# Adding the attention shift one batch ahead on GpSimd, behind VectorE's expert rows, in a transformer block with experts

## The chip, the cores and the metric

One NeuronCore of a Trainium2 chip. Its engines run their own instruction queues and meet through semaphores: TensorE (PE in the profile, weight loads PEld), VectorE (DVE), ScalarE (ACT), GpSimd (POOL), and SyncE (SP), which here only issues DMAs. The metric is the device time of one launch in microseconds.

## The reference

```python
mod = (silu(c) @ wmod)                      # per batch: sa, ca, ga, sb, cb, gb, 128 each
h = layernorm(x) * (1 + ca) + sa            # x: 8 batches x 1024 tokens x 128
x = x + ga * attention(h)                   # exp(tanh((hW+b) h^T * 1/|i-j|)), no diagonal, row-normalised, times h
h = layernorm(x) * (1 + cb) + sb
x = x + gb * ffn(h)                         # 8 experts, top 2 of 8, hidden 512, and one shared expert
```

Attention is applied to the normalised rows, and because the row weights sum to one the shift sa can be added afterwards: the kernel keeps x in SBUF (`res`), adds `ga*sa` to it (the shift), and later adds the scaled attention sum.

## The kernel before

**Tiling.** A batch is 128 partitions x 8 groups of 128 features (G = 8), so an elementwise instruction over a batch is 128x1024 f32. `res` holds all eight batches in SBUF. The attention part is a loop over batches b = 0 to 7, written out by hand for each engine; the expert part comes after it and runs over 47 tiles of sorted rows.

**One batch of attention.** Eight score tiles t, each 128 keys x 1024 queries. TensorE makes the scores, VectorE weighs them by distance (`weigh(b, t)`, L1238, one input in PSUM and one in SBUF, signals `score_used`), ScalarE takes tanh (L873) and exp (L875, `exp_done`), TensorE multiplies with the values (L1868, `value_step`). Between these, in a fixed order on each queue, lies the work of neighbouring batches:

- VectorE in batch b: `weigh` 0 and 1, `attend(b-1)` (L1247, takes the sums from PSUM), `take_ranks(b-2)` (L1308 and L1309; the latter adds two SBUF tensors of eight elements a partition), `scale_attended(b-1)` (L1256, L1257, L1260), `split_h` (L1188), `weigh` 2, `add_attended(b-1)` (L1269, which waits for `shift_added`), `moments_2(b-1)` (L1121, L1125), `split_h`, `weigh` 3, `split_q`, `normalise_2(b-1)` (L1225, waits for the second rstd), `weigh` 4, `assign(b-2)` (up to L1333, which signals `slots_ready`), `weigh` 5, `rows_for_experts(b-1)` (L1355 and L1359, the latter signals `ln2_h`; from b = 3 on), `weigh` 6 and 7, `shift_1(b+3)` (L1135, b = 3 and 4), `moments_1(b+4)` (b = 2 and 3), `choose(b-1)` (L1275, L1278, the searches L1282, and L1284) and `count_chosen` (L1290 to L1298).
- TensorE in batch b: scores 0 and 1, the last two value products of batch b-1, `ranks(b-2)` (L1889, L1890: once a batch), scores 2 and so on.
- GpSimd in batch b: `rstd_1(b+3)` in batches 3 and 4 (L528, and the pow L530; `ALU.pow` with -0.5), `add_shift(b)` (L596), then sixteen row scatters, each an indirect DMA issued by GpSimd (L622, "sends"), paced by `score_used` and `exp_done`. After the fifth comes `rstd_2(b-1)` (L600, and the pow L602), which VectorE's `normalise_2` waits for. Sends 0 to 7 carry rows of batch b-3, sends 8 to 15 rows of batch b-2; send 8 waits for `slots_ready`. In batch 2 GpSimd also makes the expert rows of batch 1 (L610, L617); from batch 3 on VectorE does.

`add_shift(b)` waits for `ln1_xhat` of batch b (ScalarE has read `res` for the normalised rows), which is over one batch earlier, and releases `shift_added`, which `add_attended(b)` needs in batch b+1. In the kernel before, `add_shift(b)` stands at the head of batch b for b = 2 to 6, and `add_shift(7)` in batch 6 between sends 11 and 12.

Of the kernel before, what the change touches and what calls it, by code (L numbers as in the profile page):

```python
# [35 lines left out]
B, S, D = 8, 1024, 128  # L36
G = S // P
# [80 lines left out]
def adaln_moe(nc, x, c_t, wmod, w_att, b_att, wg, packs, out):  # L118
    with ExitStack() as ctx:
# [6 lines left out]
        def sem(name):  # L126
            return ctx.enter_context(nc.semaphore(name))
# [185 lines left out]
        score_used = sem("score_used")  # L313
# [12 lines left out]
        ln2_h = sem("ln2_h")  # L326
# [196 lines left out]
        def _(pool):  # L523
            def rstd_1(b0, b1):

                pool.wait_ge(ln1_moments, b1)
                rs = rstd[:, b0 * G:b1 * G]
                nc.gpsimd.tensor_scalar(rs, moments[:, b0 * G:b1 * G, 1], EPS_LN, None, ALU.add).then_inc(ln1_pool_step, b1 - b0)  # L528
                pool.wait_ge(ln1_pool_step, b1)
                nc.gpsimd.tensor_tensor(rs, rs, minus_half[:, 0:(b1 - b0) * G], ALU.pow).then_inc(ln1_rstd, b1 - b0)  # L530
# [58 lines left out]
            def add_shift(b):  # L589

                pool.wait_ge(ln1_xhat, b + 1)
                if b == 0:
                    pool.wait_ge(ln1_half, 1)
                    pool.wait_ge(mod_loaded, 16)
                r = res[:, b * G:b * G + G, :]
                nc.gpsimd.tensor_tensor(r, r, mod[:, b:b + 1, 0, :].to_broadcast([P, G, D]), ALU.add).then_inc(shift_added, 1)  # L596

            def rstd_2(b):
                pool.wait_ge(ln2_moments, b + 1)
                nc.gpsimd.tensor_scalar(rstd2[:, :], moments2[:, :, 1], EPS_LN, None, ALU.add).then_inc(ln2_pool_step, 1)  # L600
                pool.wait_ge(ln2_pool_step, b + 1)
                nc.gpsimd.tensor_tensor(rstd2[:, :], rstd2[:, :], minus_half[:, 0:G], ALU.pow).then_inc(ln2_rstd, 1)  # L602

            def scale_rows(b):

                pool.wait_ge(ln2_xhat, b + 1)
                wait(pool, scattered[b % 2], 16 * 2 * G * (b // 2))
                wait(pool, second_rows, b - 1)
                scale = mod[:, b:b + 1, 3, :].to_broadcast([P, G, D])
                nc.gpsimd.tensor_tensor(rows_1[b % 2][:, :, 0:D], xhat2[:, :, :], scale, ALU.mult).then_inc(ln2_mod_step, 1)  # L610

            def shift_rows(b):

                pool.wait_ge(ln2_mod_step, b + 1)
                shift_ = mod[:, b:b + 1, 2, :].to_broadcast([P, G, D])
                to = rows_1[b % 2][:, :, 0:D]
                nc.gpsimd.tensor_tensor(to, to, shift_, ALU.add).then_inc(ln2_h, 1)  # L617
# [25 lines left out]
            def send_step(b, t, i):  # L643

                groups = sends(b, t)
                if i < len(groups):
                    send_one(*groups[i])
# [46 lines left out]
            def second_batch(b):  # L694
                rstd_2(b - 1)
                scale_rows(b - 1)
                shift_rows(b - 1)
                rstd_1(4, AHEAD)

            def batch(b, par):  # L700
                if b == 0:
                    rstd_1(2, 3)
                    add_shift(0)
                    rstd_1(3, 4)
                    add_shift(1)
                    return
                if b == 1:
                    return second_batch(b)
                if b == B - 1:
                    return last_batch(b)  # L710
                if AHEAD <= b + 3 < B:
                    rstd_1(b + 3, b + 4)
                pool.wait_ge(score_used, G * b + 1)
                add_shift(b)
                send_step(b, 0, 0)
                pool.wait_ge(exp_done, G * b + 1)
                send_step(b, 0, 1)
                pool.wait_ge(score_used, G * b + 2)
                send_step(b, 1, 0)
                pool.wait_ge(exp_done, G * b + 2)  # L720
                send_step(b, 1, 1)
                pool.wait_ge(score_used, G * b + 3)
                send_step(b, 2, 0)
                rstd_2(b - 1)
                if b < 3:
                    scale_rows(b - 1)
                pool.wait_ge(exp_done, G * b + 3)
                send_step(b, 2, 1)
                pool.wait_ge(score_used, G * b + 4)
                send_step(b, 3, 0)  # L730
                pool.wait_ge(exp_done, G * b + 4)
                send_step(b, 3, 1)
                pool.wait_ge(score_used, G * b + 5)
                send_step(b, 4, 0)
                pool.wait_ge(exp_done, G * b + 5)
                send_step(b, 4, 1)
                pool.wait_ge(score_used, G * b + 6)
                send_step(b, 5, 0)
                pool.wait_ge(exp_done, G * b + 6)
                send_step(b, 5, 1)  # L740
                if b < 3:
                    shift_rows(b - 1)
                pool.wait_ge(score_used, G * b + 7)
                if b == B - 2:
                    add_shift(b + 1)
                send_step(b, 6, 0)
                pool.wait_ge(exp_done, G * b + 7)
                send_step(b, 6, 1)
                pool.wait_ge(score_used, G * b + 8)
                send_step(b, 7, 0)  # L750
                pool.wait_ge(exp_done, G * b + 8)
                send_step(b, 7, 1)
# [9 lines left out]
            modulation()  # L762
            rstd_1(1, 2)
            batches(pool, batch)
            order = iter([(B - 3, m) for m in range(3 * (G - FIRST), 2 * G)] + [(b, m) for b in (B - 2, B - 1) for m in range(2 * G)])

# [1453 lines left out]
```

## Time and profile before

| | us |
|---|---|
| three runs, median (lowest to highest) | 642.19 (642.18 to 644.39) |
| the profiled execution, its own time | 641.25 |
| span of its profile | 639.5 |
| busy in the span: PE, DVE, ACT, POOL | 613.3, 459.0, 406.3, 350.3 |
| granted TensorE clock, mean | 0.992 |
| attention part, batches 0 to 7 | about 17 to 275 |
| shift addition L596, eight times | 2.36 to 2.40 each |

A row of the timeline has: start in us from the span's start, duration in us, engine, line, operation, output<-inputs by the program's names, shapes, and in brackets the idle time before it with what ended it. On VectorE the recorded start of an instruction lies some 0.08 us before the recorded end of the one ahead of it when they follow without a gap. A row of the chain of waits has start, duration and what the end of the program depended on in that stretch.

### The profile page before, as it was taken

Reading aid. Unit: us, or ns where it says so; the run is one execution under the profiler, and the core shown is the slowest. Engines: PE = TensorE matmul, PEld = TensorE weight load, DVE = VectorE, ACT = ScalarE, POOL = GpSimd, SP = SyncE. Lnnn points to the kernel's source line nnn. Section 1 sums busy time; section 2 is a strip of 40 time slices with the busy share of each in tenths; the row PEclk is TensorE's granted clock in tenths of the full one; section 3 lists DMA queues with packets and bytes.
Section 4 is the critical chain, followed back from the end, with each engine's and each line's share of the span. In section 5 each row is a group of like instructions: output and inputs, shape, how many; then the busy total and the mean of one; then the engine's idle time right before and its main releaser. Section 6 shows DMA issues by size and latency. Waiting matters only on the chain.

```text
span 639.5 us, 13351 instructions
## 1 busy us (share of the span) xinstructions
PE 613.3 (96%) x4339; PEld 557.5 (87%) x4339; DVE 459.0 (72%) x1425; ACT 406.3 (64%) x647; POOL 350.3 (55%) x347
## 2 busy tenths in 40 slices
PE   7899999999999998969999999999999999999997
PEld 5788898788888887858999999999999999998897
DVE  7869798999989896966842676665556544452598
ACT  3698778778787876725565656665555656463551
POOL 5450526867666666665763565566656556466100
PEclk8999999999999999988999999999999999999999
DMA  7500000110111111110752555567666566521793
GB/s 295 196 14 1 2 2 18 34 35 30 34 34 35 34 35 38 39 46 25 243 168 83 180 180 182 184 187 213 182 205 192 183 189 191 177 68 31 268 403 128
DMA packets 30031, 76.46 MB, mean 120 GB/s; under 512 B 7142, under 2 KB 11646, under 8 KB 29856
## 3 DMA queue, kind: packets, MB, share of 16 engines
q1 hardware_dynamic: 20624, 58.49, 28.1%
q0 software_dynamic: 8640, 16.93, 7.9%
q8 instruction: 23, 0.38, 0.3%
q10 hardware_dynamic: 720, 0.47, 0.2%
q14 instruction: 24, 0.20, 0.1%
HBM read 53.53 MB, written 23.24 MB: 120 GB/s over the span
## 4 chain that ended last, share of the span: by engine, by line
PE 60%; DVE 22%; ACT 5%; issue 5%; POOL 3%; another core or an unknown queue 3%; DMA 1%; POOLq 0%; SPq 0%; DVEq 0%; ACTq 0%
PE value L2060 24%; PE score L1840 8%; PE score L1842 8%; PE score L1841 8%; PE value L1868 6%; DVE work L1238 4%; DVE rows_all L1225 2%; DVE stats L1121 2%; PE value L2108 2%; PE misc L1882 2%; ACT work L873 2%; DVE rows_all L1260 2%; ACT work L875 2%; POOL rstd L602 1%
## 5 line engine op out<-in xcount | busy, mean ns | idle before, releaser
L817 POOL DMA_INDIRECT rows_z<-tile_y,tags x138 | 142.4, 1032 | 101.1 <-issue 43.7
L1840 PE MATMUL score<-h_hi,h_lo 128*128 128x512 f32 (+1 forms) x252 | 94.4, 374 | 0.3 <-ACT work L904 0.2
L1868 PE MATMUL value<-w_ring,work 128*128 128x129 f32 x768 | 93.2, 277 | 0.8 <-ACT work L875 0.3
L1868 PEld LDWEIGHTS value<-w_ring,work 128*128 128x128 f32 x768 | 89.8, 192 | 4.7 <-ACT work L875 2.0
L873 ACT ACTIVATE work<-work 128x1024 f32<-128x1024 f32 x64 | 67.3, 1052 | 38.3 <-DVE work L1238 36.2
L1842 PE MATMUL score<-h_hi,h_lo 128*128 128x512 f32 (+1 forms) x252 | 89.4, 355 | 0.0
L904 ACT ACTIVATE work<-score,w_ring 128x512 f32<-128x512 f32 (+1 forms) x96 | 53.2, 617 | 55.7 <-PE score L1842 41.8
L622 POOL DMA_INDIRECT rows_x<-work,slot x64 | 65.7, 1027 | 35.0 <-issue 16.9
L1238 DVE TENSOR_TENSOR work<-score,lw 128x1024 f32<-128x1024 f32 x64 | 76.6, 1215 | 5.0 <-remote 2.3
L1841 PE MATMUL score<-h_hi,h_lo 128*128 128x512 f32 (+1 forms) x220 | 76.4, 347 | 0.0
L2060 PE MATMUL value<-w_ring,work 128*128 128x128 f32 x640 | 75.4, 275 | 0.0
L2060 PEld LDWEIGHTS value<-w_ring,work 128*128 128x128 f32 x640 | 73.3, 192 | 0.0
L875 ACT ACTIVATE work<-work 128x1024 f32<-128x1024 f32 x64 | 67.8, 1060 | 2.0
L904 ACT ACTIVATE work<-score,rows_all 128x256 f32<-128x256 f32 (+1 forms) x92 | 44.4, 550 | 36.3 <-PE score L1842 33.4
L904 ACT ACTIVATE work<-score,w_shared 128x512 f32<-128x512 f32 x64 | 40.2, 686 | 42.7 <-PE score L1842 23.0
L1840 PE MATMUL score<-q_hi,h_lo 128*128 128x512 f32 x128 | 55.3, 432 | 5.5 <-DVE work L1238 4.5
L2060 PE MATMUL value<-rows_all,work 128*128 128x128 f32 x464 | 55.4, 275 | 0.0
L2060 PEld LDWEIGHTS value<-rows_all,work 128*128 128x128 f32 x464 | 53.6, 192 | 0.1
L1842 PEld LDWEIGHTS score<-h_hi,h_lo 128*128 128x128 f32 x252 | 47.7, 189 | 6.7
L1840 PEld LDWEIGHTS score<-h_hi,h_lo 128*128 128x128 f32 x252 | 47.9, 190 | 6.0 <-issue 0.8
L2060 PEld LDWEIGHTS value<-w_shared,work 128*128 128x128 f32 x384 | 46.1, 197 | 5.1 <-issue 4.4
L1842 PE MATMUL score<-q_hi,h_hi 128*128 128x512 f32 x128 | 50.4, 394 | 0.0
(282 smaller groups left out, 1208.4 us busy)
## 6 DMA issues: line engine op xcount, KB each, us to landing
w_ring<-packs SPq DMA_DIRECT2D x24, 578.0 KB
rows_all<-packs SPq DMA_DIRECT2D x23, 578.0 KB
lw<-rows_x SPq DMA_DIRECT2D x24, 260.0 KB
res<-x SPq DMA_DIRECT2D x8, 512.0 KB, 6.5
h_t<-rows_z SPq DMA_DIRECT2D x3, 1024.0 KB, 11.7
mod<-mod_rows SPq DMA_DIRECT2D x1, 2560.0 KB, 8.8
rows_z<-tile_y,tags POOLq DMA_INDIRECT x142
rows_all<-rows_z SPq DMA_DIRECT2D x2, 1024.0 KB, 13.2
```

The costliest lines, as they stand in the source:

```text
L622: nc.gpsimd.indirect_dma_start(rows_x[:, :], bass.IndirectOffsetOnAxis(ap=slot[b % 2][:, k, g:g + 1], axis=0), (rows_1, rows_2)[k][b % 2][ ...
L817: nc.gpsimd.indirect_dma_start(rows_z[:, :], bass.IndirectOffsetOnAxis(ap=tags[pos][:, k, 0:1].bitcast(I32), axis=0), tile_y[par][:, k, :] ...
L873: nc.scalar.activation(prob[:, t % 4, :], prob[:, t % 4, :], ACT.Tanh).then_inc(tanh_done, 1)
L875: nc.scalar.activation(prob[:, t % 4, :], prob[:, t % 4, :], ACT.Exp).then_inc(exp_done, 1)
L904: ins = nc.scalar.activation(hidden[par][:, c, 0:rows], score[:, c, 0:rows], ACT.Relu, bias=w[:, B1_AT + c:B1_AT + c + 1])
L1121: ins = nc.vector.bn_stats(st[:, g, :], res[:, bass.ds(b * G + g, 1), :].rearrange("p o d -> p (o d)"))
L1238: nc.vector.tensor_tensor(prob[:, t % 4, :].rearrange("p (h n) -> p h n", h=2), score[:, 2 * (t % 2):2 * (t % 2) + 2, :], lw[:, at:at + S] ...
L1840: nc.tensor.matmul(out, a_lo, b_hi, start=True, stop=False)
L1841: nc.tensor.matmul(out, a_hi, b_lo, start=False, stop=False)
L1842: return nc.tensor.matmul(out, a_hi, b_hi, start=False, stop=True)
L1868: ins = nc.tensor.matmul(value[:, s // 3, c0:c0 + D + 1], prob[:, t % 4, s * P:(s + 1) * P], normal[b % 3][:, t, :], start=(t == 0 and s % ...
L2060: ins = nc.tensor.matmul(bank[:, k * D:(k + 1) * D], hidden[part][:, c, k * P:(k + 1) * P], w[:, W2_AT + c * D:W2_AT + (c + 1) * D], start ...
```

## The change

GpSimd's queue only. The shifts of batches 0, 1 and 2 stay. The shift of batch 3 is added in batch 2 between sends 11 and 12, behind the shift of the expert rows (L617) and the wait for the seventh score. The shifts of batches 4 to 7 are added in batches 3 to 6, at the same place between sends 11 and 12, behind a wait for `ln2_h` of count b (VectorE has made the expert rows of batch b-1), and ahead of the wait for the seventh score.

```diff
                 pool.wait_ge(score_used, G * b + 1)
-                add_shift(b)
+                if b == 2:
+                    add_shift(b)
                 send_step(b, 0, 0)
...
                 send_step(b, 5, 1)
                 if b < 3:
                     shift_rows(b - 1)
+                    pool.wait_ge(score_used, G * b + 7)
+                else:
+                    pool.wait_ge(ln2_h, b)
+                if b < B - 1:
+                    add_shift(b + 1)
                 pool.wait_ge(score_used, G * b + 7)
-                if b == B - 2:
-                    add_shift(b + 1)
                 send_step(b, 6, 0)
```

## Rows read from the trace of the kernel before

**Rows 1.** Timeline of PE: the ranks matmul, once in batches 3 to 6.
```profile
117.17 0.29 PE L1889 MATMUL misc<-prefix,before 128*128 128x8 f32 x2
...
151.22 0.29 PE L1889 MATMUL misc<-prefix,before 128*128 128x8 f32 x2
...
184.20 0.29 PE L1889 MATMUL misc<-prefix,before 128*128 128x8 f32 x2
...
216.15 0.29 PE L1889 MATMUL misc<-prefix,before 128*128 128x8 f32 x2
```

**Rows 2.** Chain that ended last, in order of time, batches 3 and 4.
```profile
121.54 1.92 DVE rows_all L1260 x7
...
152.91 1.12 DVE carry L1309
...
169.84 2.05 PE value L1868 x16
```

**Rows 3.** All of line L1309: duration ns min/median/max, first and last start.
```profile
L1309 DVE TENSOR_TENSOR carry<-carry,prefix x8: 159/174/2062, 86.2 to 313.2; 128x8 f32<-128x8 f32 x8
```

**Rows 4.** Timeline of POOL, end of batch 2 and batch 3.
```profile
109.30 2.20 POOL L617 TENSOR_TENSOR work<-work,mod 128x1024 f32<-128x1024 f32 x1
...
118.53 2.36 POOL L596 TENSOR_TENSOR res<-res,mod 128x1024 f32<-128x1024 f32 x1
121.06 1.10 POOL L622 DMA_INDIRECT rows_x<-rows_all,slot  x1 [0.18 <-issue]
...
125.20 1.96 POOL L622 DMA_INDIRECT rows_x<-rows_all,slot  x1 [0.30 <-issue]
127.47 0.96 POOL L622 DMA_INDIRECT rows_x<-rows_all,slot  x1 [0.30 <-issue]
128.78 0.58 POOL L600 TENSOR_SCALAR rstd<-moments 128x8 f32<-128x8 f32 x1 [0.35 <-DVE moments L1125]
...
142.05 0.96 POOL L622 DMA_INDIRECT rows_x<-work,slot  x1 [0.30 <-issue]
```

**Rows 5.** Timeline of POOL, batches 0, 1, 4 and 6.
```profile
37.15 1.67 POOL L530 TENSOR_TENSOR rstd<-rstd,minus_half 128x8 f32<-128x8 f32 x1
...
62.71 0.24 POOL L600 TENSOR_SCALAR rstd<-moments 128x8 f32<-128x8 f32 x1 [21.53 <-DVE moments L1125]
...
151.62 2.38 POOL L596 TENSOR_TENSOR res<-res,mod 128x1024 f32<-128x1024 f32 x1
...
238.96 0.96 POOL L622 DMA_INDIRECT rows_x<-row,slot  x1 [0.30 <-issue]
239.94 2.38 POOL L596 TENSOR_TENSOR res<-res,mod 128x1024 f32<-128x1024 f32 x1
```

**Rows 6.** Timeline of DVE, batch 0 and batches 2 to 4.
```profile
37.91 0.68 DVE L1188 TENSOR_TENSOR h_lo<-tile_y,h_hi 128x512 fp32r<-128x512 f32 x1
...
112.57 0.15 DVE L1284 TENSOR_TENSOR gap<-top_v 128x8 f32<-128x8 f32 x1
...
117.44 1.36 DVE L1247 TENSOR_TENSOR rows_all<-value,rows_all 128x387 f32<-128x387 f32 x3 [0.79 <-PE value L1868]
...
118.85 2.06 DVE L1309 TENSOR_TENSOR carry<-carry,prefix 128x8 f32<-128x8 f32 x1
...
125.11 1.22 DVE L1269 TENSOR_TENSOR res<-res,rows_all 128x1024 f32<-128x1024 f32 x1
...
128.60 0.66 DVE L1188 TENSOR_TENSOR h_lo<-tile_y,h_hi 128x512 fp32r<-128x512 f32 x1
...
137.09 0.17 DVE L1333 TENSOR_SCALAR token_no<-token_no 128x8 f32<-128x8 f32 x1
...
143.10 0.16 DVE L1135 SCALAR_TENSOR_TENSOR shift<-moments,rstd 128x8 f32<-128x8 f32 x1
...
152.83 1.20 DVE L1309 TENSOR_TENSOR carry<-carry,prefix 128x8 f32<-128x8 f32 x1
...
178.25 0.23 DVE L1275 COPY logits<-misc 128x64 f32<-128x64 f32 x1 [1.99 <-PE misc L1882]
```

## Prediction

> **What bounds the kernel now.** I read the page first: the busy shares name TensorE, but those are means over an attention part and an expert part, and the change touches only the attention part of batches 2 to 6. So the next view is the timeline of TensorE, taken at one matmul that occurs once a batch (the ranks, L1889). The reader is to see its spacing [rows 1]: 34.05 us from batch 3 to 4, 32.98 from 4 to 5, 31.95 from 5 to 6. If 31.95 is the pace that the rest of the work allows, the two earlier batches lose 2.10 and 1.03 us, 3.13 together. That is the cap of what removing anything in them can bring.
>
> Who loses them is in the chain of waits [rows 2]: from 121.54 it runs over VectorE, with one odd piece, 1.12 us for the carry addition L1309, and comes back to TensorE's values at 169.84. The VectorE timeline then shows L1309, eight elements a partition, taking 2.06 us in batch 3 and 1.20 in batch 4 [rows 6], against 0.17 in the median of its eight runs [rows 3]. What ran beside it is in the GpSimd timeline: the shift addition L596 from 118.53 to 120.89 [rows 4] and from 151.62 to 154.00 [rows 5]. L1309 ends at 120.91 and 154.03, within 0.03 us of L596's end both times. So a VectorE instruction with both inputs in SBUF stands still until GpSimd's long addition is over. Cost: 2.06 - 0.16 = 1.90 us and 1.20 - 0.16 = 1.04 us, close to the losses of 2.10 and 1.03. In the later batches GpSimd has no rstd of a later batch ahead of L596, which then comes and goes before L1309.
>
> **The change, part by part.** The eight additions stay; none is added. Moved are shifts 3, 4, 5, 6 and 7.
>
> *Shift 7.* It stood behind the wait for the seventh score already, and GpSimd arrives there late: its last send ends at 239.92 and L596 starts at 239.94 [rows 5]. The new wait (VectorE's expert rows) is over before. Nothing changes: 0.
>
> *Shifts 5 and 6* leave the head of batches 5 and 6 and go behind the sixth pair of sends in batches 4 and 5. No L1309 is blocked there now; the sends get 2.4 us later at the tail and 2.4 earlier at the head. The tail has room: the sends of one batch are read by TensorE only much later. 0.
>
> *Shift 3* leaves 118.53 and goes behind L617, which ends at 111.50 [rows 4]; it then runs to 113.9. GpSimd is busy without a gap from there to 121.06, so this only permutes its queue: four sends to 118.9, the rstd of batch 6 to 120.9, first send of batch 3 at 121.06 as before. Removed: L1309's 1.90 us. Added: VectorE's L1284 at 112.57 [rows 6] has both inputs in SBUF and now waits until 113.9, 1.3 us. Of that 0.79 is covered by VectorE's idle wait for TensorE ahead of L1247 at 117.44 [rows 6]; 0.5 stays. VectorE's scaling L1260 is thus 1.9 - 0.5 = 1.4 us earlier. But what is late next is GpSimd. VectorE's normalise_2 (L1225) needs the second rstd, and this stands behind five sends. Now VectorE's moments arrive at 128.7, and the last of the five sends ends at 128.43 [rows 4]: a margin of 0.3. With moments at 127.3, GpSimd is the later one. Its five sends at a pitch of 0.96 + 0.30 from 121.06 would end at 127.1. Yet a send beside the VectorE addition L1269 (125.11 to 126.33) took 1.96 instead of 0.96 [rows 4, 6], so 1.0 is added, and smaller brushes of 0.1 to 0.4 by the other two-input instructions. I lay the five beside VectorE's new times: 0.1 + 0.1 + 1.04 + 0 + 0.4, end 128.75. The rstd then runs free of L1188, which in the run before stretched L600 to 0.58 (128.78, beside L1188 from 128.60; free 0.24) [rows 4 to 6]. L600 to 129.0 and the pow of 1.67 behind it [rows 5] to 130.8, against 129.36 and 131.1 before. Gain of batch 3: 0.35 us, between 0 (the sends brush more) and 0.75 (the last one doesn't).
>
> *Shift 4* leaves 151.62 and goes behind the sixth pair of batch 3, whose last send ends at 143.01 [rows 4]. Removed: 1.04 us at L1309 of batch 4. The same test of GpSimd: L596 from 143.03 to 145.4, four sends to 150.4, the rstd of batch 7 to 152.4, all 0.35 earlier, instead of the 154.00 at which L596 ended; five sends at the pitch of 1.26 and a brush or wait of 1.5 to 2 then end at 159.9 to 160.3. The moments came 7.8 us behind the end of L1309 in batch 3 (120.91 to 128.7); in batch 4 it now ends at 154.03 - 1.04 - 0.35 = 152.6, so they come at 160.4. So here VectorE leads, barely, and the 1.04 is kept. L1309 itself is clear of GpSimd: the rstd of batch 7 is over at 152.0 and L1309 comes at 152.83 - 0.35 = 152.5.
>
> *The new neighbour.* Behind that last send (143.01) the addition starts after 0.02 us, at 143.03. VectorE's shift_1 (L1135), both inputs in SBUF, starts at 143.10 [rows 6], and both hang on the same release, the slots of L1333 at 137.09, so their distance stays 0.07 us whatever moved earlier. Who takes the port first? L600 started at 128.78, was let go when L1188 ended at 129.26, and ended at 129.36; with 0.24 for a free one it asked for the port about 0.14 us after its start. So L596 would ask near 143.17, and L1135 in 143.10 to 143.26. This can't be decided from the trace. If VectorE is first, GpSimd waits 0.1 us: nothing. If GpSimd is first, L1135 waits to 145.4, costs 2.17 us, and behind it on VectorE are the moments of batch 7, the choice, and the scores of batch 4. The same pair meets in batch 4 (shift 5), but there VectorE then waits 1.99 us for TensorE anyway, until 178.25 [rows 6], and the addition is over at 178.4: 0 to 0.2, in slack.
>
> **Sum.** Likeliest: 0.35 + 1.04 = 1.4 us less. The profiled execution took 641.25 (span 639.5), so it would take 639.9. The median of the runs is 642.19, 0.94 above it: 640.8.
>
> **Rule and row.** Rows: GpSimd's pow L530 ran from 37.15 to 38.82, and VectorE's L1188 at 37.91, both inputs in SBUF, took its usual 0.68 [rows 5, 6]; so GpSimd's eight-element pow doesn't hold VectorE to its end. The Trainium skill (SBUF — State Buffer, Who interferes with whom) says that the one to issue first holds the shared port pair for the whole instruction. L1309 agrees; the pow doesn't. By that rule L1260 would stand behind the pow in batch 3 (rival 3).
>
> **Rivals.**
> 1. *L1135 loses the race (slower than before).* Place: batch 3, behind the last of the twelfth send. +2.17 at L1135, -1.04 at L1309 of batch 4, -0.35 of batch 3: +0.8 us, 643.0; without the 0.35, 643.3. It decides once GpSimd asks for the port before VectorE does, a matter of 0.05 us. For it: L596's earlier recorded start. Against: L1135 touches only eight elements.
> 2. *The sends don't slow GpSimd.* Then VectorE's whole 1.4 of batch 3 arrives: -(1.4 + 1.04) = -2.5, 639.7. Against: the send of 1.96 us. The same page infers that a two-input VectorE addition leaves descriptor generation alone; by it this would be the result, and the 1.96 beside L1269 speaks against it.
> 3. *The pow takes the place of the addition.* The rstd of batch 6 now lies at 119.2 to 120.9, where L596 lay. If it holds L1260 until then, batch 3 gains 0 and batch 4 its 1.04: 641.2. Against: 37.91 above.
> 4. *Nothing moves:* the pace of batches 3 and 4 has another cause, and L1309's wait lies in slack: 642.2. Against: L1309 is on the chain.
>
> **Chances and range.** Forecast 0.45, rival 1 0.34, rival 2 0.06, rival 3 0.07, rival 4 or a mixture 0.08. Range 639.5 to 643.6: from rival 2 to rival 1 without its 0.35, with 0.2 to 0.3 for the scatter of a median; about 0.8 is in it. The range of the forecast itself: 640.4 (0.75 in batch 3) to 641.2 (0). A measurement of this kernel tells from no change about 0.5%, 3.2 us; that is more than the cap of 3.13, and slower by as much would take rival 1 with its 2.17 unpaid and more. Faster by over 0.5% 0.05, within 0.88, slower by over 0.5% 0.07.
>
> **What would show it.** L1309 at 0.16 to 0.25 in batches 3 and 4. L1284 in batch 2 at 1.4 us. The spacings of L1889: 33.7 from batch 3 to 4, 31.95 from 4 to 5, with the forecast; 33.7 and 34.1 with rival 1. L1135 of batch 3: 0.16, or 2.3. The send beside L1269 in batch 3 again near 2 us, and L602 there no more than 0.4 us earlier against L1889. The prediction fails if another two-input instruction of VectorE meets the addition (the searches L1282 just ahead of L1284, which no row shows beside one), or if TensorE's clock dips elsewhere.

## The result, and the profile after

| | before, beside it | after | ratio, 95% interval |
|---|---|---|---|
| median (lowest to highest), us | 643.29 (642.18 to 644.64) | 652.13 (650.73 to 652.85) | 1.0134 [1.0102, 1.0166] |

The change makes the kernel slower by 1.3%, some 9 us. The forecast was 1.4 us less, with 643.6 as the upper end. The profiled execution took 652.85 us (span 651.1, mean granted clock 0.980) against 641.25 (639.5, 0.992). Medians here and below hold all executions of a kernel, while the ratios leave out the disturbed ones. In the kernel after every line number behind the diff is 4 higher: L1893 is the ranks matmul that was L1889, L1313 the carry addition L1309, L1139 the shift computation L1135, L1251 the line that takes the attention sums (L1247).

First the timeline of PE after, at the ranks matmul, batches 3 to 7, against [rows 1]:

```profile
118.29 0.29 PE L1893 MATMUL misc<-prefix,before 128*128 128x8 f32 x2
...
152.68 0.36 PE L1893 MATMUL misc<-prefix,before 128*128 128x8 f32 x2 [0.20 <-DVE prefix L1302]
186.45 0.29 PE L1893 MATMUL misc<-prefix,before 128*128 128x8 f32 x2
...
221.69 0.29 PE L1893 MATMUL misc<-prefix,before 128*128 128x8 f32 x2
...
258.73 0.28 PE L1893 MATMUL misc<-prefix,before 128*128 128x8 f32 x2
```

| from rank to rank, us | 3 to 4 | 4 to 5 | 5 to 6 | 6 to 7 |
|---|---|---|---|---|
| before | 34.05 | 32.98 | 31.95 | 31.56 |
| after | 34.39 | 33.77 | 35.24 | 37.04 |
| more | 0.34 | 0.79 | 3.29 | 5.48 |

The 1.12 us by which batch 3 already starts later (118.29 against 117.17) lie ahead of the change's reach: the ranks of batch 2 are already 1.11 us later (85.72 against 84.61). The batches that the prediction argued over cost 1.1 us. The loss is in batches 5 and 6, 8.8 us, which it priced at nothing.

The timeline of DVE after shows the part that was foreseen, and the loss, against [rows 6]:

```profile
113.65 1.30 DVE L1288 TENSOR_TENSOR gap<-top_v 128x8 f32<-128x8 f32 x1
...
120.08 0.16 DVE L1313 TENSOR_TENSOR carry<-carry,prefix 128x8 f32<-128x8 f32 x1
...
131.49 2.17 DVE L1229 TENSOR_SCALAR rows_all<-res,moments,rstd 128x128 f32<-128x128 f32 x8 [1.11 <-POOL rstd L602]
...
143.44 2.35 DVE L1139 SCALAR_TENSOR_TENSOR shift<-moments,rstd 128x8 f32<-128x8 f32 x1
...
156.11 0.21 DVE L1313 TENSOR_TENSOR carry<-carry,prefix 128x8 f32<-128x8 f32 x1
...
189.48 1.36 DVE L1251 TENSOR_TENSOR rows_all<-value,w_ring 128x387 f32<-128x387 f32 x3 [2.70 <-remote]
...
226.10 1.36 DVE L1251 TENSOR_TENSOR rows_all<-value,rows_all 128x387 f32<-128x387 f32 x3 [4.95 <-remote]
```

L1313 is free now, 0.16 instead of 2.06 us in batch 3 and 0.21 instead of 1.20 in batch 4; L1288 pays 1.30. L1139 takes 2.35 us instead of 0.16. And VectorE stands still for 2.70 and 4.95 us ahead of L1251, which waits for the last value product of the batch. "Remote" means that the profile finds no instruction that ended when the wait did. The timeline of PE says that the product was finished long before:

```profile
182.88 3.74 PE L1872 MATMUL value<-w_ring,work 128*128 128x129 f32 x32
...
188.06 0.39 PE L1846 MATMUL score<-q_hi,h_hi 128*128 128x512 f32 x1
191.11 0.63 PE L1827 MATMUL misc<-ident,w_ring 128*128 128x128 f32 x4 [2.67 <-DVE place L1312]
```

The value products end at 186.62 by the records, but the signal of the last one arrives at 189.45, and VectorE goes on at 189.48. In the semaphore events of the trace, which carry the time at which each signal arrives, the rank signal of batch 5 comes 3.21 us behind the recorded end of its matmul and that of batch 6 3.94 us; before, both were 0.01 us behind. The score signal that follows the rank signal comes 0.74 us after it in batch 5, and 0.08 us after it in batch 6 (226.22 against 226.14), while the matmuls between the two take 1.49 us by their records both times. So it looks as if TensorE worked on time and its signals came late. The ends of matmuls are modelled in this trace, so a real standstill inside TensorE for a part of the time isn't excluded. Signals of VectorE and ScalarE aren't late at these places.

What GpSimd does there is in the timeline of POOL after, batches 4 and 5, and 5 and 6, against the pattern of [rows 4]:

```profile
178.29 2.38 POOL L596 TENSOR_TENSOR res<-res,mod 128x1024 f32<-128x1024 f32 x1
180.84 0.98 POOL L622 DMA_INDIRECT rows_x<-row,slot  x1 [0.17 <-issue]
182.13 0.96 POOL L622 DMA_INDIRECT rows_x<-row,slot  x1 [0.30 <-issue]
183.39 0.96 POOL L622 DMA_INDIRECT rows_x<-row,slot  x1 [0.30 <-issue]
184.66 0.96 POOL L622 DMA_INDIRECT rows_x<-row,slot  x1 [0.31 <-issue]
185.92 0.96 POOL L622 DMA_INDIRECT rows_x<-rows_all,slot  x1 [0.31 <-issue]
188.10 0.96 POOL L622 DMA_INDIRECT rows_x<-rows_all,slot  x1 [1.22 <-ACT work L879]
...
213.53 2.39 POOL L596 TENSOR_TENSOR res<-res,mod 128x1024 f32<-128x1024 f32 x1
216.08 0.98 POOL L622 DMA_INDIRECT rows_x<-work,slot  x1 [0.17 <-issue]
...
223.74 0.96 POOL L622 DMA_INDIRECT rows_x<-work,slot  x1 [0.30 <-issue]
```

The addition in the tail makes GpSimd 2.4 us late, so the four sends of the tail wait for nothing any more. At the head of the next batch, where the addition used to stand between tail and head, the sends go straight on. Five follow each other without a pause at 180.84 to 186.88, and seven at 216.08 to 224.70. In batch 5 the signal of the last but one value product, due at 184.83, arrives at 187.94, 1.06 us after the run; those behind it, the last value product's at 189.45 among them, come while two more sends go (188.10 to 190.33). In batch 6, where none follow, the last value, rank and score signals arrive together at 226.08 to 226.22, 1.4 to 1.5 us after the run.

The view by windows of 2 us shows what comes behind it. Its columns are the window and its length, the busy time of PE, PEld, DVE, ACT and POOL (with the number of instructions), the granted clock of TensorE as a share of full speed, the DMA share and GB/s:

```profile
188.00:190.00 2.00, 0.45 (x2) 0.02 (x1) 0.52 (x2) 0.00 (x0) 1.59 (x2) 1.00 0.10 33
190.00:192.00 2.00, 0.89 (x8) 0.92 (x9) 1.93 (x10) 0.22 (x1) 0.33 (x1) 0.96 0.10 33
192.00:194.00 2.00, 2.00 (x11) 2.00 (x11) 2.00 (x8) 1.97 (x3) 0.00 (x0) 0.50 0.00 0
194.00:196.00 2.00, 2.00 (x10) 1.78 (x10) 2.00 (x3) 1.97 (x3) 0.00 (x0) 0.69 0.00 0
196.00:198.00 2.00, 2.00 (x11) 1.65 (x10) 1.97 (x9) 1.97 (x3) 1.22 (x2) 1.00 0.00 0
```

TensorE is idle for 2.67 us, and from 191.8 to 195.3 the clock is 1.2 instead of 2.4 GHz; in batch 6 TensorE is idle for 4.04 us, and the clock is at the lower level for 6.8 us. The value products that start at 191.58 take 3.40 us where the same sixteen took 1.95 in the kernel before, 1.45 us more. So each wait is paid a second time behind it. Slack takes up a part: VectorE's waits of 2.70 and 4.95 us come with distances that are 3.29 and 5.48 us longer. The Trainium skill (TensorE: Matmul & The Clock Gate, HAM oscillation — how this bites in real kernels) says that idle gaps of TensorE bring the lower clock and that it is paid behind each gap; the rows agree.

### The profile page after: what moved, and what is told of

It reads as the page before. It is cut to its first block, busy times and chain, and to the rows that moved or that the text cites. A ratio compares the mean times of both kernels' runs of the same rounds, so it can differ in the third digit from the quotient of the medians.

```text
span 651.1 us, 13355 instructions
## 1 busy us (share of the span) xinstructions
PE 618.0 (95%) x4339; PEld 562.3 (86%) x4339; DVE 461.6 (71%) x1425; ACT 406.3 (62%) x647; POOL 347.9 (53%) x347
## 4 chain that ended last, share of the span: by engine, by line
PE 59%; DVE 24%; issue 5%; POOL 5%; ACT 3%; another core or an unknown queue 2%; DMA 1%; DVEq 0%; POOLq 0%; SPq 0%
PE value L2064 23%; PE score L1844 8%; PE score L1846 8%; PE score L1845 8%; PE value L1872 6%; DVE work L1242 4%; POOL rows_x L622 2%; PE value L2112 2%; DVE rows_all L1229 2%; DVE stats L1125 1%; DVE top_i L1286 1%; PE misc L1827 1%; PE misc L1886 1%; DVE rows_all L1251 1%
## 5 line engine op out<-in xcount | busy, mean ns | idle before, releaser
L1872 PE MATMUL value<-w_ring,work 128*128 128x129 f32 x768 | 94.6, 279 | 0.6 <-ACT work L879 0.3
L1872 PEld LDWEIGHTS value<-w_ring,work 128*128 128x128 f32 x768 | 91.6, 195 | 3.9 <-ACT work L879 1.7
L622 POOL DMA_INDIRECT rows_x<-work,slot x64 | 63.9, 999 | 44.6 <-issue 16.6
L2064 PEld LDWEIGHTS value<-w_ring,work 128*128 128x128 f32 x640 | 73.3, 192 | 0.0
L1845 PE MATMUL score<-q_lo,h_hi 128*128 128x512 f32 x128 | 50.3, 393 | 0.0
```

The lines of the kernel that those rows point to most:

```text
L622: nc.gpsimd.indirect_dma_start(rows_x[:, :], bass.IndirectOffsetOnAxis(ap=slot[b % 2][:, k, g:g + 1], axis=0), (rows_1, rows_2)[k][b % 2][ ...
L1845: nc.tensor.matmul(out, a_hi, b_lo, start=False, stop=False)
L1872: ins = nc.tensor.matmul(value[:, s // 3, c0:c0 + D + 1], prob[:, t % 4, s * P:(s + 1) * P], normal[b % 3][:, t, :], start=(t == 0 and s % ...
L2064: ins = nc.tensor.matmul(bank[:, k * D:(k + 1) * D], hidden[part][:, c, k * P:(k + 1) * P], w[:, W2_AT + c * D:W2_AT + (c + 1) * D], start ...
```

## The experiments

The kernels ran on four chips in turn, called A to D here; which of them, if any, the result above is from isn't known. Each was compared with the kernel before on its own chip, and only so are the times to be read:

| runs | chip | before there, us | kernel, us | ratio, 95% interval |
|---|---|---|---|---|
| 1 only shift 3 ahead | A | 641.63 | 641.60 | 1.0007 [0.9989, 1.0024] |
| 2 only shift 4 ahead | A | 641.63 | 644.14 | 1.0039 [1.0014, 1.0065] |
| 3 only shifts 5 and 6 ahead | A | 641.63 | 648.75 | 1.0125 [1.0101, 1.0150] |
| 4 all ahead, one send later | A | 641.63 | 644.12 | 1.0060 [1.0038, 1.0081] |
| 5 shifts 5 and 6 in halves | B | 641.95 | 642.62 | 1.0019 [0.9996, 1.0042] |
| 6 run 3 with a held send | B | 641.95 | 644.02 | 1.0026 [1.0005, 1.0046] |
| 7 shifts 5 and 6 tiny | B | 641.95 | 642.19 | 1.0006 [0.9982, 1.0031] |
| 8 a run of six sends, nothing moved | B | 641.95 | 644.93 | 1.0041 [1.0020, 1.0061] |
| 9 shift 7 at its head | C | 631.88 | 635.37 | 1.0054 [1.0034, 1.0075] |
| 10 run 9, shifts 3 and 4 ahead and later | C | 631.88 | 633.10 | 1.0016 [1.0003, 1.0029] |
| 11 the changed kernel again | C | 632.65 | 632.37 | 1.0012 [0.9994, 1.0030] |
| 12 the kernel before again | C | 632.65 | 632.44 | 0.9999 [0.9978, 1.0019] |
| 13 run 9 again | C | 632.65 | 635.30 | 1.0048 [1.0031, 1.0064] |
| 14 run 10 again | C | 632.65 | 633.25 | 1.0015 [1.0003, 1.0027] |
| 15 the changed kernel, third time | D | 647.00 | 663.10 | 1.0236 [1.0187, 1.0286] |
| 16 shifts 3 and 4 ahead, one send later | D | 647.00 | 646.92 | 0.9995 [0.9974, 1.0016] |
| 17 run 16, shift 7 in halves | D | 647.00 | 643.66 | 0.9960 [0.9937, 0.9984] |

**Which part costs (runs 1 to 4).** Theory A: the sends close up into a run, and that makes TensorE's signals late. Theory B: the wait of L1139 sets the later batches back. In runs 1 to 3 only some shifts are moved, with the change's place and waits:

```diff
                 pool.wait_ge(score_used, G * b + 1)
-                add_shift(b)
+                if b not in (5, 6):
+                    add_shift(b)
...
+                if b + 1 in (5, 6):
+                    if b < 3:
+                        pool.wait_ge(score_used, G * b + 7)
+                    else:
+                        pool.wait_ge(ln2_h, b)
+                    add_shift(b + 1)
                 pool.wait_ge(score_used, G * b + 7)
```

(3 or 4 in place of 5, 6 in the other two.) In run 4 all additions of the change stand behind send 12 instead of send 11. What was expected:

> Only the shift of batch 3 goes ahead (into batch 2). The result of the whole change is 8.8 us slower than before, and its trace shows three things: L1135 (L1139 after) of batch 3 stands 2.35 us beside the moved addition; TensorE's value_step and rank signals of batches 5 and 6 come some 3 and 4 us behind the recorded matmuls while GpSimd issues five to seven row sends in a row; and then the granted clock falls to one half. Theory A (runs of sends): what costs is that the addition no longer stands between the sends of one batch's end and the next one's head; this one here isn't such a place, since the rstd of batch 6 still stands there, so 0 to 0.5 us less than before. Theory B (VectorE's block): what costs begins with L1135 beside the addition in batch 3; shift 3 doesn't touch it, so the same 0 to 0.5 us less. L1309 of batch 3 falls from 2.06 to 0.2 us, L1284 of batch 2 rises from 0.15 to 1.3.

> Only the shift of batch 4 goes ahead (into batch 3). Theory A: plus 2.2 us at L1135, minus 1.04 at L1309 of batch 4, so about 1.1 us slower than before and no more; the clock doesn't fall in batches 5 and 6. Theory B: VectorE's block alone starts the later losses, so most of the 8.8 us.

> Only the shifts of batches 5 and 6 go ahead. Theory A: nearly the whole loss, 7 to 9 us slower than before, with TensorE's signals late at the start of batches 5 and 6 and the clock at one half behind it. Theory B: L1135 of batch 4 is blocked, in slack; 0 to 0.5 us, no fall of the clock.

> The whole change, but each addition one send later (behind the seventh pair's first send), so that L1135 is over before it starts. Theory A: the sends behind it are still followed by the next batch's without a break, so still 6 to 8 us slower than before. Theory B: L1135 is free, so 1 to 2 us faster than before.

Shift 3 alone changes nothing that can be measured in the time. Shift 4 alone costs 2.5 us, where 1.1 was expected (the interval, 0.9 to 4.2 us, holds both). Its L1142 (L1135 in the kernel before) takes 2.35 us at 143.84, the later batches keep their distances of 31.91 and 31.57 us, and no rank signal of batches 5 and 6 is late: the wait of that line alone doesn't start the loss, and theory B falls. Shifts 5 and 6 alone cost 7 us, most of the 8.8. Timeline of DVE in run 3:

```profile
187.23 1.36 DVE L1254 TENSOR_TENSOR rows_all<-value,w_ring 128x387 f32<-128x387 f32 x3 [2.68 <-remote]
...
223.33 1.36 DVE L1254 TENSOR_TENSOR rows_all<-value,rows_all 128x387 f32<-128x387 f32 x3 [4.95 <-remote]
```

The same two waits as in the changed kernel to 0.02 us, from rank signals 3.17 and 3.94 us late. Run 4 leaves one send fewer behind each addition, so that four sends go in a row in batch 5 and four in batch 6, and the same waits shrink to 1.07 and 2.08 us. Its time fits neither theory: A wanted 6 to 8 us more than before, B 1 to 2 less, and it is 2.5 more. Theory A was too high for a run that is only one or three sends shorter.

**The run of sends, or the missing addition (runs 5 to 8).** Theory C: it costs that the addition is gone from the head, whatever the sends do. Run 5 adds four groups ahead and four at the head. Run 6 is run 3 with one more wait. Run 7 leaves the additions at their heads but adds only eight elements a partition of shifts 5 and 6. Run 8 moves no addition and only holds sends back, so that they go in a row:

```diff
 run 6, at the head of batches 5 and 6
+                if b in (5, 6):
+                    pool.wait_ge(score_used, G * b + 2)
                 send_step(b, 0, 0)
 run 8, in the tail of batches 4 and 5
+                if b in (4, 5):
+                    pool.wait_ge(score_used, G * b + 8)
                 send_step(b, 5, 0)
```

> Shifts 5 and 6 cut into two halves of four groups each, one half ahead (between sends 11 and 12 of the batch before), the other at the head of its own batch. Theory A (five or more sends in a row, with no other work between them, make TensorE's signals late): the half at the head parts the sends of the tail, four in a row, from those of the head. No late rank signal (lag under 1 us, where the kernel with shifts 5 and 6 ahead had 3.17 and 3.94), no half clock in batches 5 and 6, time within 1 us of the kernel before, 641 to 643. Theory C (what costs is that the addition is gone from the head, whatever the sends do): half of it is gone, so about half of the 7 us that both cost, 645.

> Shifts 5 and 6 ahead as in the run that cost 7 us, and in batches 5 and 6 the first send of the batch is held until VectorE has weighed the second score tile, with nothing else put in its place. Theory A: the hold parts the run of sends, four in the tail and then a pause of some 2 us, so the rank signal is on time and the time is 641 to 644. If a pause is not enough and it takes other work of GpSimd, or if the missing addition itself costs (theory C): 648 to 649 and a lag of 3 to 4 us as before the hold.

> The shift additions of batches 5 and 6 stay at the head of their batch but add only eight elements a partition (the rest of these two shifts is left out). GpSimd has 2.2 us less work there and nothing more in the tail. Theory A: without the late addition in the tail the sends go at the pace of the scores, no run of five forms across the border, no late signal: 641 to 642. Theory C: the long addition is gone from the head as in the changed kernel, so the same loss: 648 to 649.

> All additions stay where the kernel before has them; in batches 4 and 5 sends 10 and 11 are held until VectorE has weighed the eighth score tile, so that the last six sends of the batch go in a row, up to the addition at the head of the next. Theory A: the run alone, with no addition moved, makes the rank signals of batches 5 and 6 late by 3 us or so; each costs about 3 us, and the clock may fall behind it: 646 to 649. Theory C: nothing was moved; only the carry addition is brushed for 0.4 us: 642 to 643.

Runs 5 and 7 are level with the kernel before, and no rank signal of batches 5 and 6 is late in run 5; for run 7 the trace shows it for batch 5 and the undisturbed distances (31.94 and 31.55 us) for both. In run 5 a piece of work of 1.28 us, with 1.55 us from the send ahead of it to the send behind it, is enough. Run 6 is a pause alone. Timeline of POOL in run 6, batches 5 and 6:

```profile
185.38 0.96 POOL L622 DMA_INDIRECT rows_x<-rows_all,slot  x1 [1.94 <-DVE work L1247]
...
216.62 0.96 POOL L622 DMA_INDIRECT rows_x<-work,slot  x1 [1.07 <-DVE work L1247]
```

The pause of 1.94 us mends batch 5 (rank signal 0.01 us late). That of 1.07 us in batch 6 doesn't: the rank signal is 2.52 us late and VectorE waits 2.87 us. So a pause can do what work does; whether 1.07 us of work would be enough wasn't tried. Theory A wanted run 8 at 646 to 649 and signals 3 us late; it got 644.93. Timelines of POOL and DVE in run 8:

```profile
177.25 0.96 POOL L622 DMA_INDIRECT rows_x<-row,slot  x1 [3.47 <-DVE work L1240]
...
183.56 0.96 POOL L622 DMA_INDIRECT rows_x<-row,slot  x1 [0.31 <-issue]
184.54 2.40 POOL L596 TENSOR_TENSOR res<-res,mod 128x1024 f32<-128x1024 f32 x1
```

```profile
186.01 1.36 DVE L1249 TENSOR_TENSOR rows_all<-value,w_ring 128x387 f32<-128x387 f32 x3 [2.12 <-PE value L1870]
```

The value signals arrive at 185.83 and 185.99, 1.3 and 1.5 us after the sixth send ended at 184.52, and VectorE stands still for 2.12 us in batch 5 and 2.15 in batch 6, with every addition at its head. The run alone does it; theory C (642 to 643 here, 648 to 649 for run 7) falls. By the records the signal that L1249 waits for is only 1.30 us late and the rank signal 1.0, since here the run ends before the matmuls do; the first of the two value signals, due at 182.91, is 2.92 us late. That suggests that the price goes by how far the run reaches past them. The kernel before bears it out: it has five sends in a row in the middle of its batches too (138.04 to 144.28, 171.04 to 177.28, 203.02 to 209.26). The signal of the logits matmul L1882 behind them comes at 145.28, 178.22 and 210.20, 0.94 to 1.00 us after the run, but the matmul itself ends only then, and the signal is 0.7 to 0.8 us late. The number of sends alone doesn't set the price.

**A better version, and a surprise (runs 9 to 14).** In the kernel before, shift 7 already stands in the tail. Its timelines of POOL and DVE, not shown so far:

```profile
239.94 2.38 POOL L596 TENSOR_TENSOR res<-res,mod 128x1024 f32<-128x1024 f32 x1
242.48 0.99 POOL L622 DMA_INDIRECT rows_x<-row,slot  x1 [0.17 <-issue]
...
248.86 0.96 POOL L622 DMA_INDIRECT rows_x<-rows_all,slot  x1 [0.30 <-issue]
```

```profile
249.63 1.23 DVE L1238 TENSOR_TENSOR work<-score,lw 128x1024 f32<-128x1024 f32 x1 [2.14 <-remote]
```

Six sends in a row and a wait of 2.14 us for a score signal, with the rank signal 2.81 us late: the kernel before has the same late signals in batch 7. Run 9 is to part that run of sends by putting shift 7 at the head of batch 7, and run 10 adds shifts 3 and 4 ahead, behind send 12.

> The kernel before with one move the other way: shift 7, which stood in batch 6 between sends 11 and 12, goes to the head of batch 7. Theory A: in the kernel before, this addition makes GpSimd late too, and the six sends behind it (242.48 to 249.82) run on into batch 7, where the rank signal lagged 2.81 us and VectorE stood still 1.10 and 2.14 us. With the addition between the tail's sends and the head's, the signals are on time and VectorE's two waits shrink: about 2 us less, 640 where the kernel before takes 642. If the long run of fourteen sends at the end of batch 7 then starts later and takes it back: no change.

> Shift 7 at the head of batch 7 as well, and of the change only shifts 3 and 4 ahead, each one send later than the change puts it (behind send 12), where the run with all additions one send later had no long wait of the shift computation in batch 3 and distances of 33.53 and 31.97 us between ranks against 34.05 and 32.98. Shifts 5 and 6 stay at their heads, so no run of sends forms. Expected: 0.5 and 1.0 us from batches 3 and 4 on top of what shift 7 at its head gives, 3 to 3.5 us together by theory A, 638.5; if the move of shift 7 gives nothing, 640.5.

Both missed: 3.5 and 1.2 us slower. But they ran on chip C, where the kernel before takes 631.9 us, and in neither trace is any TensorE signal more than 0.5 us late, not even behind fourteen sends. There is nothing to gain there, and the addition at the head of batch 7 holds a two-input instruction of VectorE for 2.42 us (L1290 at 247.59). So the changed kernel, the kernel before and both of these were run again:

> The changed kernel once more, unaltered, beside the kernel before. In the last call the kernel before took 631.9 us, 10 us less than on the two chips before it, and no TensorE signal in either kernel's trace came late, not even behind a run of fourteen sends. Theory A, as widened: whether signals come late behind a run of sends is a property of the chip. If this chip's kernel before takes about 642: lags of 3 to 4 us in batches 5 and 6 and 9 to 10 us more than before. If it takes about 632: no lag, and only the work of VectorE and GpSimd is left, with the shift computation of batch 3 held for 2.35 us: 0 to 2 us more than before. Theory D (the lags belong to the kernel and the last two runs only had a lucky order): lags here whatever the level of the kernel before.

> The kernel before itself, for a trace on this chip. If it takes about 642: the rank signal of batch 7 is 2.8 us late and that of the batch after 3.7 us. If it takes about 632: no signal late, spacings of the ranks in batches 6 and later near 31.5, 30.7 and 27, and all the 10 us lie behind 240 us. The ratio to itself shows what a comparison can tell: within 0.3% of one.

> Shift 7 at the head of batch 7 again. On a chip whose signals come late behind runs of sends, theory A gives 1 to 3 us less than the kernel before, since the run of six sends is parted; on one where they don't, 3 us more as in the last call, where the addition at the head held VectorE's two-input instruction for 2.42 us at 247.59.

> Shift 7 at the head, shifts 3 and 4 ahead behind send 12, again. With late signals: 2 to 4 us less than before; without: 0 to 1.5 us more, as in the last call.

It was chip C again, and on it the changed kernel is level with the kernel before, 1.0012 [0.9994, 1.0030]. Theory D (the late signals belong to the kernel) falls. Runs 13 and 14 repeat 9 and 10, as expected without late signals (2.7 and 0.6 us more than before). Timelines of POOL and DVE in run 11:

```profile
176.80 2.39 POOL L596 TENSOR_TENSOR res<-res,mod 128x1024 f32<-128x1024 f32 x1
179.36 0.98 POOL L622 DMA_INDIRECT rows_x<-row,slot  x1 [0.17 <-issue]
...
184.45 0.95 POOL L622 DMA_INDIRECT rows_x<-rows_all,slot  x1 [0.32 <-DVE work L1242]
```

```profile
142.66 2.36 DVE L1139 SCALAR_TENSOR_TENSOR shift<-moments,rstd 128x8 f32<-128x8 f32 x1
...
185.22 1.35 DVE L1251 TENSOR_TENSOR rows_all<-value,w_ring 128x387 f32<-128x387 f32 x3
```

The same run of five sends, the same hold of L1139, and L1251 starts without a wait. From rank 5 on the kernels keep the same pace: 32.01, 31.50 and 29.78 us in run 11, 32.12, 31.76 and 29.78 in run 12.

**A fourth chip (runs 15 to 17).** Run 16 is run 10 without the move of shift 7. Run 17 adds shift 7 in two halves, one at its old place and one at the head of batch 7:

```diff
                 if b == B - 2:
-                    add_shift(b + 1)
+                    add_half(b + 1, 0)
                 send_step(b, 6, 0)
+                if b + 1 in (3, 4):
+                    add_shift(b + 1)
...
             def last_batch(b):
                 pool.wait_ge(score_used, G * b + 1)
+                add_half(b, 4).then_inc(shift_added, 1)
                 send_step(b, 0, 0)
```

> The changed kernel a third time. Late signals come on some chips (kernel before near 642) and not on the last one (near 632). If the kernel before takes about 642 here: 9 us more than it, with rank signals 3 to 4 us late in batches 5 and 6. If about 632: within 0.3% of it and no late signal. A mix (before at 642 and the changed kernel without late signals, or the reverse) would speak against the chip as the cause.

> Of the change only shifts 3 and 4, each behind send 12 of the batch before instead of behind send 11; 5 to 7 as in the kernel before. On the last chip this with shift 7 at its head stood 2.0 us below shift 7 at its head alone (633.25 against 635.3), so without that head 2 us less than the kernel before: ratio 0.997. The same is expected where signals come late, since no run of sends is lengthened.

> As the run with shifts 3 and 4 behind send 12, and shift 7 in two halves of four groups, one where it stood (between sends 11 and 12 of batch 6), one at the head of batch 7. Where signals come late, the half at the head parts the run of six sends: 1 to 2 us less than without it. Where they don't: the half holds VectorE's two-input instruction by up to 1.2 us and nothing is gained, 0 to 1.5 us more than without it.

On chip D the kernel before takes 647.0 us and the changed kernel 663.1, 2.4% or 16 us more, where 9 was expected; its rank signals are 4.05 and 4.02 us late. Timeline of DVE in run 15:

```profile
191.91 1.36 DVE L1251 TENSOR_TENSOR rows_all<-value,w_ring 128x387 f32<-128x387 f32 x3 [4.21 <-remote]
...
229.57 1.36 DVE L1251 TENSOR_TENSOR rows_all<-value,rows_all 128x387 f32<-128x387 f32 x3 [5.04 <-remote]
```

Here even five sends cost 4.21 us, against 2.70. Run 16 gains nothing (0.9995); 0.997 had been expected. Behind the six sends of batch 7 its VectorE waits 3.63 us, as the kernel before presumably does on this chip (it has no trace from there). Run 17 parts those six. Timelines of DVE at that place, first run 16, then run 17:

```profile
249.89 1.22 DVE L1241 TENSOR_TENSOR work<-score,lw 128x1024 f32<-128x1024 f32 x1 [3.63 <-PE score L1845]
```

```profile
245.15 1.23 DVE L1248 TENSOR_TENSOR work<-score,lw 128x1024 f32<-128x1024 f32 x1 [2.06 <-PE score L1852]
246.51 1.31 DVE L1301 TENSOR_TENSOR hot<-expert_no,top_f 128x64 f32<-128x64 f32 x1
```

The rank signal, 2.94 us late in run 16, is on time (0.01), though VectorE's wait only falls to 2.06 us. The time falls from 646.92 to 643.66 us, more than the 1 to 2 us that were expected, and is below the kernel before at 0.9960 [0.9937, 0.9984]. It costs a hold of 1.31 us at L1301, so on a chip like C it should gain nothing; it wasn't run there.

## Why the prediction was wrong

**The step that failed** is the one on shifts 5 and 6: "the sends get 2.4 us later at the tail and 2.4 earlier at the head. The tail has room: the sends of one batch are read by TensorE only much later. 0." Who reads the sent rows doesn't matter. The two halves of the first sentence together close the gap between tail and head, and behind the run of five to seven sends TensorE's signals come 3 to 4 us late (run 3); where the run is parted they don't (run 5), and where it is made without moving an addition they do (run 8, up to 2.9 us). Measured: 3.3 and 5.5 us in the two batches, 7 us for both shifts alone on chip A, nothing that shows on chip C. The price went with the chip, which no reading of one trace could tell. That there was a price could be read: the "remote" wait of 2.14 us behind the six sends of batch 7 stood in the trace of the kernel before, behind the one addition that already stood where the change puts the others. The prediction looked at shift 7 only to say that it doesn't move; it was the sample of what the place costs.

**The race at L1135** went to rival 1. L596 starts at 143.37, L1139 0.07 us later at 143.44, and is held for 2.35 us (2.17 was the forecast's price, 2.19 measured over its 0.16). It is so in all three traces of the changed kernel, in batches 3 and 4, and in run 2. The step gave this 0.34 and should have given it more: the earlier recorded start decided, and the 0.14 us that L600 was thought to need before it asks for the port didn't save L1135. The Trainium skill (SBUF — State Buffer, Who interferes with whom) says that issue order decides who is held, and the traces agree here. The Trainium skill also has it there, of the SBUF ports, that TensorE never waits on anyone; the late signals of runs 3, 8 and 15 don't decide that, but they say that an engine waiting for TensorE can be held past the recorded end of its matmul.

**Rival 1's sum** was +0.8 us. In the kernel after, batches 3 and 4 cost 0.34 + 0.79 = 1.13 us. The hold in batch 4 is in slack, as the prediction said: in run 3 L1142 takes 2.34 us at 176.13, and the distance from rank 4 to 5 stays 32.97. The hold in batch 3 falls into both distances, so that rival 1's 33.7 and 34.1 came as 34.39 and 33.77. On chip C, where nothing else is in the way, the rank of batch 5 is 0.51 us later in run 11 than in run 12 (184.98 against 184.47), and the whole kernel 0.12% or 0.8 us slower (0.0012 × 632.65), with an interval from -0.4 to +1.9. The sum fits, but can't be told from zero, so that it fits to the tenth is luck.

**Batch 3's terms** came as worked out: L1309 free (0.16), L1284 held for 1.30, the send beside L1269 stretched (1.68 us at 124.80), and GpSimd the later one, since VectorE's L1229 now waits 1.11 us for the rstd [rows 4, 6]. The gain of 0.35 can't be read off by itself, because the hold of L1139 falls into the same distance: +0.34 in the changed kernel, +0.10 on chip C (34.06 against 33.96). With the hold taken out by placing the addition one send later, the distance is 33.53 in run 4 and 33.49 in run 16, 0.5 under the 34.05 of before. Run 1, which moves shift 3 alone to the place of the change, has 33.37, 0.68 less. So 0.35 was on the low side, within the 0 to 0.75 that was given.

**Batch 4's term**, 1.04 us, was right in kind. In run 4 the distance is 31.97 and in run 16 32.01, against 32.98. The 1.5 us of both don't show in the time of run 16, though (0.9995, at most 0.26% less). In the comparison of runs 13 and 14, which differ by these two moves alone, they do: 635.30 against 633.25. Where they go on chip D isn't settled, since the kernel before has no trace from that chip.

**Rivals 2, 3 and 4** aren't borne out: the sends did slow GpSimd down, the work did move, and the pow didn't hold VectorE (in batch 3 it runs from 120.25 to 121.92, and L1264 beside it, from 120.59 on, takes its usual 2.19 us). None of the rivals held the loss; rival 1 had the sign, but short by a factor of ten and more where signals come late.

**Open.** What makes TensorE's signals late isn't known. It needs indirect DMAs in a row, most of its late signals arrive 1 to 1.5 us after them, and it differs from chip to chip. A load of instructions doesn't explain it: in the changed kernel the trace has none between 179.02 and 202.51 us, and the signals of batch 5 are late from 184.83 to 190.91. Each chip was met on one or two occasions only, so that something else that differed between the occasions isn't excluded. Whether sends from another queue would do the same wasn't tried.

## What to carry to other kernels

When work is moved along a queue, look at both ends for what it stood between: here an addition parted two groups of DMA sends, and the closed-up run cost three times the two waits that were to be removed (8.8 us against 1.90 + 1.04), though on one chip of four nothing. If one member of a group already stands at the new place, read what happens around it before taking it for proof that the place is free; a wait whose releaser the profile can't name is a cost and belongs in the sum. Where a filler parts such a run, splitting it in halves can keep the run parted (runs 5 and 17). And compare on more than one chip before a gain or a loss of a per cent is called the kernel's.

## What the runs showed of the hardware

- Behind unbroken runs of GpSimd's indirect DMAs (0.96 us each, 1.26 us apart) TensorE's signals arrive late. Six in a row: 2.81 us late on the rank signal in the kernel before, seven: 3.94 in the changed kernel. Five: 3.21 there, 4.05 on chip D. The lateness isn't set by the number alone: behind five in the middle of a batch the signal of L1882 is only 0.7 to 0.8 us late, since its matmul ends after the run. Most of those that are held come in 1.0 to 1.5 us after the run ends. VectorE's and ScalarE's signals were on time. A break of 1.55 us with 1.28 us of other work, or a pause of 1.94 us, takes it away; a pause of 1.07 us left 2.52 us.
- It goes with the chip: no signal over 0.5 us late on chip C, and the kernel before takes 631.9 us there, 641.6 to 647.0 on the three others.
- Idle stretches of TensorE of 2.67 and 4.04 us were followed by 3.4 and 6.8 us at the lower clock (1.2 instead of 2.4 GHz).
- A VectorE instruction of eight elements with two SBUF inputs, that starts 0.07 us behind GpSimd's addition of 128x1024, takes 2.35 us, until the addition is over (six of six times in the three traces of the changed kernel).
